# Delta loop of one core: a turn takes two sequences of two tiles instead of one

## What is computed

```python
def step(S, inp):
    qt, kt, vt, gt, bt = inp
    S = S * jnp.exp(gt)[..., None, None]
    pred = jnp.einsum('bhk,bhkv->bhv', kt, S)
    S = S + jnp.einsum('bhk,bhv->bhkv', kt, (vt - pred) * bt[..., None])
    o = jnp.einsum('bhk,bhkv->bhv', qt, S)
    return (S, o)
...
x = x + _L0_attn_ref(_layernorm(x, axis=-1), ...)   # the delta rule: conv, silu, scan, gate, W_o
x = x + _L0_ffn_ref(_layernorm(x, axis=-1), ...)    # one routed expert of 8 and a shared one
x = x + _L1_attn_ref(_layernorm(x, axis=-1), ...)   # attention in a window of 64
x = x + _L1_ffn_ref(x, ...)                         # full attention, then 2 of 8 experts
```

## Time and profile before

| | us |
|---|---|
| median of 3 runs | 7086.48 (7085.24 to 7096.07) |
| the profiled execution | 7100.42 |
| its span, first to last instruction | 7098.7 |
| delta loop, first turn's end to last turn's end | 477.0 to 4436.5, 31 turns |

### The profile page before, as it was taken

One profiled execution on the slowest core, in us unless ns is written; L12 is line 12 of the kernel. 1 busy time (PEld: TensorE's weight loads), 2 busy tenths in 40 slices (PEclk: granted clock), 3 DMA queues, 4 the chain that ended last, 5 costly groups with the idle time before them and its releaser, 6 DMA issues. The chain is left out here.

```text
span 7098.7 us, 188681 instructions
## 1 busy us (share of the span) xinstructions
PE 5892.0 (83%) x68007; PEld 4415.0 (62%) x68008; DVE 3695.3 (52%) x7201; ACT 3275.5 (46%) x7091; POOL 2495.1 (35%) x2342
## 2 busy tenths in 40 slices
PE   2299999999999999999999999675888778886587
PEld 2166666666666666666666666464666556665486
DVE  3055555555555555555555555554444456665433
ACT  1155555555555555555555555132333235553165
POOL 1244444445444444445444444332000000002554
PEclk8599999999999999999999999897999989997588
DMA  2930000000000000000000000111000000001124
GB/s 79 302 101 2 2 2 2 2 2 2 2 2 2 2 2 2 2 2 2 2 2 2 2 2 2 35 44 47 0 0 0 2 1 0 0 0 31 37 60 120
DMA packets 98480, 160.40 MB, mean 23 GB/s; under 512 B 19204, under 2 KB 81476, under 8 KB 95300
## 3 DMA queue, kind: packets, MB, share of 16 engines
q10 hardware_dynamic: 10688, 74.89, 3.4%
q1 hardware_dynamic: 73124, 50.74, 2.7%
q0 software_dynamic: 14080, 26.64, 1.1%
HBM read 118.03 MB, written 104.87 MB: 31 GB/s over the span
## 5 line engine op out<-in xcount | busy, mean ns | idle before, releaser
L754 PE MATMUL bank<-wc,hT 128*128 128x512 f32 x2088 | 1075.4, 634 | 72.4 <-issue 59.0
L911 PE MATMUL bank<-X,kqe 128*128 128x64 f32 x6240 | 775.8, 278 | 75.2 <-DVE rb L1393 54.6
L911 PEld LDWEIGHTS bank<-X,kqe 128*128 128x128 f32 x6240 | 727.8, 192 | 99.2 <-DVE rb L1393 70.2
L1141 ACT ACTIVATE TT<-bank 128x512 bf16<-128x512 f32 x640 | 382.1, 597 | 686.4 <-PE bank L892 684.0
L1428 DVE TENSOR_TENSOR yb<-bank,masks 128x512 bf16<-128x512 f32 x768 | 527.0, 687 | 204.4 <-PE bank L874 194.4
L754 PEld LDWEIGHTS bank<-wc,hT 128*128 128x128 f32 x2088 | 369.1, 200 | 369.5 <-issue 347.0
L1372 DVE TENSOR_TENSOR kqe<-bank,ex 128x512 f32<-128x512 f32 x520 | 335.1, 686 | 325.0 <-PE bank L820 325.0
L1235 POOL TENSOR_TENSOR qa<-qa,qt 128x512 f32<-128x512 f32 x390 | 486.8, 1269 | 35.0 <-POOL qt L1230 35.0
L1268 POOL TENSOR_SCALAR_AFFINE_SELECT kqe<-kqe 128x512 f32<-128x512 f32 x260 | 215.0, 827 | 791.7 <-DVE kqe L1372 791.7
L1141 ACT ACTIVATE T<-bank 128x512 bf16<-128x512 f32 x640 | 348.9, 595 | 272.7 <-PE bank L885 270.6
L1096 ACT ACTIVATE ex<-bank,gate_bias_all 128x128 f32<-128x128 f32 x1040 | 290.0, 372 | 374.0 <-DVE kqe L1372 183.6
(11 more groups left out here) (526 smaller groups left out, 13244.4 us busy)
## 6 DMA issues: line engine op xcount, KB each, us to landing
sent_l0f<-blank_l0f ACTq DMA_DIRECT2D x8, 4224.0 KB, 64.5
sent_l1m<-blank_l1m ACTq DMA_DIRECT2D x8, 4224.0 KB, 139.0
xin<-sent_l1m SPq DMA_DIRECT2D x139, 66.0 KB
taken_l1m<-back_l1m SPq DMA_DIRECT2D x16, 512.0 KB, 8.7
xin<-sent_l0f SPq DMA_DIRECT2D x75, 66.0 KB
decay_sums<-decay_rows SPq DMA_DIRECT2D x264, 3.0 KB
cw_stage<-in_L_attn_conv_w_dram SPq DMA_DIRECT2D x4, 1024.0 KB, 6.8
out_dram<-x_sb ACTq DMA_DIRECT2D x8, 512.0 KB, 7.4
```

What stands on the lines that cost most here:

```text
L754: mm = pe.matmul(bk[:, :], src[:, j:j + P], w["wc"][:, j, at * 512:(at + 1) * 512], start=(j == 0), stop=(j == TAPS - 1))
L911: mm = pe.matmul(bk[:, i * D0:(i + 1) * D0], lhsT(hh), rhs(hh), start=True, stop=True)
L1141: nc.scalar.activation(dst, bk[:, :].rearrange("p (h a u) -> p h a u", h=8, u=1 << l), ACT.Copy).then_inc(actb.done.sem, 1)
```

## The change

A turn now takes two sequences, four tiles written out (`U = 2 * TPB`), and the loops run 16 times instead of 32. Inside, t counts 0 to 3; what had asked for t = 1 now asks for an odd t, buffers are chosen by t % 2 as before, and addresses go by `b * U`. The semaphores' counts per turn double. No operation, no operand and no wait is added or dropped, apart from the register steps around the branch.

```diff
-    N = turns * TPB
+    U = 2 * TPB
+    N = turns * U
...
-        U = TPB
...
-        kd_ready = signal("kd_ready", 1)
-        rows_in = [signal(f"decay_rows_in{t}", 16 * NHB) for t in range(U)]
+        kd_ready = signal("kd_ready", U // 2)
+        rows_in = [signal(f"decay_rows_in{t}", 16 * NHB * U // TPB) for t in range(TPB)]
...
-        rhs_ready = signal("rhs_ready", 1)
+        rhs_ready = signal("rhs_ready", U // 2)
...
             with sp.Fori(0, turns) as b:
-                for t in range(TPB):
+                for t in range(U):
                     lone_wait(sp, actb.full.sem, actb.full.at(b, actb.uses.at(t - 1, "ex.3")), sp_passed)
-                    load(bass.ds(b * TPB + t + TPB, 1), t)
+                    load(bass.ds(b * U + t + TPB, 1), t % TPB)
...
             with pe.Fori(0, turns) as b:
-                for t in range(TPB):
-                    taps(b, hT[t], "v0", 2, 2)
+                for t in range(U):
+                    taps(b, hT[t % 2], "v0", 2, 2)
...
-                                if t == 1:
+                                if t % 2 == 1:
                                     state(b, t, G)
...
-                    if t == 1:
+                    if t % 2 == 1:
                         from_state(b, t, 0, "ks")
                         from_state(b, t, 1, "qs")
...
             with act.Fori(0, turns) as b:
-                for t in range(TPB):
+                for t in range(U):
                     right_side(b, t)
...
             with pool.Fori(0, turns) as b:
-                for t in range(TPB):
+                for t in range(U):
                     convolve(b, t + 1)
...
             with dve.Fori(0, turns) as b:
-                for t in range(TPB):
+                for t in range(U):
...
-        delta_attention(nc, c, {"wc": wc, "wq": wq, "cq": cq, "wz": wz, "wo": wo}, x_all, mr, gates, decay_rows, tiles // TPB, sendings)
+        delta_attention(nc, c, {"wc": wc, "wq": wq, "cq": cq, "wz": wz, "wo": wo}, x_all, mr, gates, decay_rows, tiles // (2 * TPB), sendings)
```

More of the change, by code:

```diff
@@ L541, in at @@
     def at(self, t, name):
-        if t == TPB:
+        if t == len(self.slots):
             return self.ahead + self.per + self.behind.index(name) + 1
-        turn, slot = divmod(t, TPB)
+        turn, slot = divmod(t, len(self.slots))
         return self.ahead + turn * self.per + sum(map(len, self.slots[:slot])) + self.slots[slot].index(name) + 1
@@ L600, in act_slot @@
             names += [f"t.{l}.0", f"t.{l}.1"] + ["h"] * (l == 4)
-            names += [f"tt.{l}.0", "s.0", f"tt.{l}.1", "s.1"] if l == 5 and t == 1 else [f"tt.{l}.0", f"tt.{l}.1"]
+            names += [f"tt.{l}.0", "s.0", f"tt.{l}.1", "s.1"] if l == 5 and t % 2 == 1 else [f"tt.{l}.0", f"tt.{l}.1"]
         names += ["tt.6.0", "tt.6.1"]
@@ L884, in join_t @@
                     hh = G * 8 + i
-                    mm = pe.matmul(bk[:, i * HALF:(i + 1) * HALF], TT[t][:, hh, :], yb[:, hh, :], start=True, stop=True)
+                    mm = pe.matmul(bk[:, i * HALF:(i + 1) * HALF], TT[t % 2][:, hh, :], yb[:, hh, :], start=True, stop=True)
                 mm.then_inc(actb.full.sem, 1)
@@ L902, in join_last @@
                     hh = G * 8 + i
-                    mm = pe.matmul(bk[0:HALF, i * HALF:(i + 1) * HALF], yb[:, hh, :], TT[t][:, hh, HALF:],
+                    mm = pe.matmul(bk[0:HALF, i * HALF:(i + 1) * HALF], yb[:, hh, :], TT[t % 2][:, hh, HALF:],
                                    start=True, stop=True)
@@ L1009, in _ @@
                     decayed(b, t)
-            b, t = turns - 1, TPB
+            b, t = turns - 1, U
             taps(b, hT[0], "v0", 2, 2)
@@ L1206, in _ @@
                          x_all[:, N + 1:N + 3, :], hTz, mr[:, :, N:N + 2], gates["bias"][:, N, :],
-                         gates["dec"][:, turns, :], kqe[1][:, :, :, :], TT[1][:, :, :]):
+                         gates["dec"][:, N // TPB, :], kqe[1][:, :, :, :], TT[1][:, :, :]):
                 last = pool.memset(zero, 0.0)
@@ L1292, in _ @@
                     lone_wait(pool, proj.full.sem, proj.full.at(b, proj.uses.at(t, "z1")), pool_passed)
-                    pool.tensor_copy(hTz, hT[t][:, TAPS - 1:]).then_inc(kept_ready.sem, 1)
+                    pool.tensor_copy(hTz, hT[t % 2][:, TAPS - 1:]).then_inc(kept_ready.sem, 1)
                     decayed(b, t)
-            b, t = turns - 1, TPB
+            b, t = turns - 1, U
             gate_o(b, t)
```

40 lines of the change are left out of this document (20 added, 20 removed).

## The result

| | before | after |
|---|---|---|
| median of 6 runs each, same job, us | 7095.01 (7085.24 to 7144.65) | 7183.95 (7169.60 to 7201.93) |
| ratio, 95% interval | | 1.0113 (1.0094 to 1.0132) |
| profiled execution, us | 7100.42 | 7184.18 |
| its span | 7098.7 | 7182.4 |
| delta loop's last branch (L965) | 4434.6 | 4467.8 |

The kernel got 1.1% slower. The prediction was 7082 with a range of 7050 to 7105, so it missed on the sign and by 102 us. Of the 83.7 us between the spans, 33 stand up to the last branch of the delta loop, which was changed, and 48 in a loop that was not touched, the third of TensorE's loops behind it. The branches of TensorE give both numbers. The rows are as the earlier trace rows: times run, ns min/median/max, first and last start.

What follows compares the result with a forecast made beforehand. TensorE was taken to bound the delta loop, with a wait at each back edge. Against the profiled 7100.42 us, -33 + 2 + 27 = -4 gave 7096, or 7082 on the median's scale; range 7050 to 7105.

Steps and rivals of the forecast that it cites:

- (1) Back edges: Delta loop on TensorE: 16 of the back edges go, 2.05 us each; 33 us saved, range 29 to 38.
- (2) ScalarE's wait: ScalarE behind the delta loop's branch: its 2.94 us issue wait lies beside TensorE's own stall; gain 0.
- (3) Longer straight code: Delta loop body doubled on every engine: same work, no instruction fetch that TensorE waits for; 0.
- (4) VectorE and GpSimd at the back edges left: Remaining 15 back edges: VectorE may miss its fetch, 0 to 9 us, taken as 2; GpSimd 0.
- (5) The clock: Delta loop: shortened turns slip against TensorE's half-clock spells; +27 us taken, from -32 to +93.
- the second rival: Delta loop slower through the clock: shortened turns mostly land badly, +59 less 31, total 7114; chance 0.17.
- The even chance of a bad odd half: Delta loop: odd half in the bad place every second time, 0.5 x 3.1 = 1.55 us a turn.
- the prediction's own chances: Clock term, delta loop: disturbed odd and even halves together cost 2.6 us a turn against 1.5 before.
- its own +35: Clock term, delta loop: 32 x 1.1 us from the half-chances, before it was lowered to +27.
- what would show it: Profile signs; for the clock: odd halves split evenly into 65.9 and 68.8 to 69.0, mean clock below 0.97.

Runs made afterwards that it cites:

- e11: Eight tiles in a turn (8 turns) plus long products moved between the odd tile's two state products, against the changed kernel; 7009 us, 0.9864 of the kernel before.
- e5: Changed kernel with 24 TensorE semaphore steps mid turn and 45 more behind the delta loop; 7142 us, 1.0099 of the kernel before.
- e9: Changed kernel with 26 TensorE semaphore steps mid turn, none behind the delta loop; 7104 us, 1.0000 of the kernel before.
- e1: Changed kernel with 69 TensorE semaphore steps once behind the delta loop; 7137 us, 1.0030 of the kernel before.
- e2: Kernel before the change with 187 TensorE semaphore steps once behind the delta loop; 7190 us, 1.0102 of the kernel before.
- e3: Changed kernel with 72 TensorE semaphore steps in the middle of its turn; 7277 us, 1.0213 of the kernel before.

## Why the prediction was wrong, point by point

**(1) Back edges, -33.** Right: 59.0 us in 31 pieces became 28.1 in 15, that is -31 inside the loop.

**(2) ScalarE's wait, 0.** Right. It is still there across the turn's end, 33.2 us in 15 pieces ahead of L1133, and TensorE's own stall covers it.

```profile
3444.58 1.06 ACT L1133 ACTIVATE rb<-v 128x1024 bf16<-128x1024 f32 x1 [2.09 <-issue]
```

**(3) Longer straight code, 0.** This step failed, with 48 us. Its argument was about the delta loop and holds there: no issue wait appeared inside the longer turn. It did not ask what the 2747 more instructions do to loops that come after them. The earlier trace rows was read as a property of L2838 (0.215 us since it is short enough), when it was a property of L2838 at that place. No rival had this. It alone takes the time out of the range: 7082 + 48 = 7130 against the 7105 of its upper end.

**(4) VectorE and GpSimd at the back edges left, +2.** Right. VectorE does miss: in the record of its instructions the one behind the branch follows 2.84 us later, in the median, instead of 0.32. The row shows no "issue", because the wait for TensorE is longer:

```profile
3446.43 1.29 DVE L1420 TENSOR_TENSOR T<-bank,mask 128x512 bf16<-128x512 f32 x2 [3.62 <-PE bank L854]
```

TensorE goes from L799 to L874 in 10.25 us, 10.21 before: 0 of the 0 to 9. GpSimd at its 271 recorded instructions did not miss, at 539 (e11) it did. The 7091 that the prediction gives as the upper end for this term is 7089 by its own sum, since 2 of the 9 us are in the 7082 already.

**(5) The clock, +27 taken from -32 to +93.** This step failed too, in its size: 66 us, between the +59 of the second rival and the upper bound. The mechanism was right: the shortened turns slipped against the spells and paid for it. What was off shows in the half turns between the first and last branch, beside their undisturbed lengths (65.9; 60.3 with a back edge, 58.2 without). The even chance of a bad odd half came true, 15 of 30 are above 65.9. But a bad one was priced at 3.1 us and cost 4.5 on average, since seven of them were of the 72.2 kind that the earlier trace rows has once: 2.3 us a pair instead of 1.55. Of the even halves 25 of 30 were disturbed, more than the half (and some of those without a back edge) that had been put in: 1.35 us a pair instead of 1.05. Together that is 3.6 us a pair where the prediction's own chances gave 2.6, against 1.5 before: 32 x 2.1 = 66.

The prediction then went below its own +35 because "a good place can be kept from turn to turn once it is found". The runs show that this is true and speaks for the other side: the place was kept by a turn of 126.2 us between spells 126.3 apart, and e5 and e9 differ by 0.3 us in a turn of four tiles and by 57 us in the loop. A turn of 250.3 us has no such fit. Every turn of after has one odd half at 65.9 and one at 68.8 to 72.3, and that repetition costs more than chance would. Of "what would show it", the split of the odd halves came out evenly, as said, but with 72.2 beside 69, and the mean clock fell from 0.97 to 0.96.

In sum: -2 ahead of the loop, -31 for the back edges and +66 for the clock make the +33 at the loop's last branch, 48 came from the place of the code, and 2.6 are spread over the rest: 83.7. Without the 48 (e1) the kernel is 0.3% slower than before, where the second rival said 7114 against 7086.5, 0.4%.

## What to carry to other kernels

Unrolling a loop moves all code behind it: look at the maximum, not the median, of every later loop's branch, and put some idle instructions behind the unrolled loop when one has become slow (69 did it here; the number hangs on where the code lies). Before a steady loop is shortened, compare the distance of its spells at half clock with its turn: where they fit, the loop is cheap by that fit, and a saving of a microsecond can cost more than it brings. The remedy that held under all three turn lengths tried here (low clock 157 to 188 us) was to remove the hole at which the clock falls, by moving long products into the wait among small ones. That alone gave 0.6%, and unrolling alone was a loss. On top of the filling, four tiles in a turn brought nothing that could be measured, and eight tiles made it 1.4%.

## What the runs showed of the hardware beside that

- Semaphore steps on TensorE started 0.15 us apart (e1, e2, e3, e5), inside the loop behind queued matmuls and behind the loop alike, though the record of one lasts 0.05 us.
- Adding 2.4 us of idle time to each of 16 turns made the loop 64 us shorter (4467.8 to 4403.8).
- A missed branch took 3.3 to 4.0 us on TensorE, and the next instruction came 3.4 us behind the branch on GpSimd (0.26 when it did not miss) and 2.8 on VectorE (0.32). TensorE's bodies of 2754 recorded instructions and more missed every time, that of 1577 only where it lay in the slow place.
- The shared-expert loop, untouched, took turns of 20.7, 23.7 or about 27.2 us, with 154 to 181 us from its first to its last branch; what decides it stays open.
